# Two attention blocks on one core: block 2's keys and values as three float32r products, scores laid out by batch, output product moved behind the next pair's scores

## Chip, cores and metric

One Trainium2 chip, one of its cores. The metric is the device time of the kernel in microseconds (us), median of three runs. Five engines work side by side, each through its own list of instructions in order, and they wait for one another by semaphores: PE (matmuls; PEld is its weight load), DVE, ACT, POOL, and SP, which here only issues DMAs.

## What is computed

32 sequences of 64 tokens, width 128. A transformer block with 16 heads of width 8 (causal self-attention, attention to a context, a feed-forward part, three layer norms) is followed by one attention block with 16 heads of width 64, a bias `f` on the scores that counts twice, an output product and a layer norm. Block 2, which the change is about, cut to what matters:

```python
x = block1(x, ctx)                                   # 3 layer norms, small heads
qh = (x @ wq + bq) / 8;  kh = ctx @ wk + bk;  vh = ctx @ wv + bv     # 16 heads x 64
scores = qh @ kh.T + f + f                           # per batch and head, 64 x 64
ctx2 = softmax(scores) @ vh
out = layernorm(ctx2 @ wo + bo + x)                  # width 128
```

All data is fp32 in memory. Wq, wk, wv of block 2 are 128 x 1024.

## The kernel before

Two sequences make a pair (128 tokens, one per partition), so there are 16 pairs. Every pair goes through three chains of steps: A (self-attention and its layer norm), B (attention to the context, its layer norm, the feed-forward part and its layer norm) and C (block 2). A of one pair, B of an earlier one and C of a still earlier one run at the same time; A is five pairs ahead of C, B two to three.

**Order.** Each engine's list is written by one function, `run`, which goes through `PLAN`: the steps of all chains and pairs, sorted by pair number plus a place from the table `TURN` (`C.e=-1.106` and so on). An engine takes from it the steps that are its own. So the table alone sets the order on every engine, and once 11 or so pairs are in flight the same rows repeat for each pair. Between engines only semaphores (`s_...`) order the work.

**Banks.** A and B have three PSUM banks each (J, E, X). Chain C has two, `C.E[0]` and `C.E[1]`, each 128 x 512 fp32, and every product of C goes through them in turn: keys (`C.k_0`, `C.k_1`), values (`C.v_0`, `C.v_1`), the transposed input (`C.x3t`), queries (`C.q_0/1`), scores (`C.e`), transposed probabilities (`C.pt_0/1`), probabilities times values (`C.zt`) and output product (`C.o_0/1`).

**Chain C, step by step** (line of the kernel in brackets):
- `C.k_g` (L455): keys. For four pairs at a time one product of a 128 x 128 slice of wk with 512 columns of the transposed context; two of them in each pair's turn, four pairs ahead of their use. `C.ks_g` (ACT, L614) adds the bias and copies into `kT`.
- `C.v_b` (L469): values of batch b, in two products with 64 rows of output each and 512 columns; `C.vs_b` (ACT, L624) copies.
- `C.x3t`, `C.q_g` (L480, L488): queries; `C.qs_g` (ACT, L646) adds bias and scales by 1/8.
- `C.e` (L503): 32 products 64 x 64 x 64. It waits for `L4.s_y`: the addition `C.y` of the pair before has read the output product out of bank 0.
- Softmax: `C.fadd_g` (DVE, L837) computes 2f + scores from PSUM, `C.max_g` (DVE, L846), `C.sub_g` (POOL, L929), `C.exp_g` (ACT, L654), `C.den_g` (DVE, L854, L856), `C.nrm_g` (POOL, L938).
- `C.pt_g` (L514), which also waits for the queries of the next pair to be out of the banks, `C.pts_g` (ACT, L663), `C.zt` (L528), `C.zts_r` (ACT, L633), `C.o_r` (L537): eight products 128 x 128 x 128 that add up in 128 columns of bank 0.
- `C.y` (DVE, L865) adds x; then the layer norm of C: `C.st` (DVE), `C.rstd` (POOL), `C.xh` (DVE), `C.gb` (POOL), `store` (SP).

The same four names with A, B and B.3 before them are the other three layer norms (L795 and L799, L896 and L898, L808, L907 and L912). `A.kblk` and `B.kblk` (POOL, L888) spread the keys of block 1 over eight heads (128 x 1024); `A.e` and `B.e` (L365) wait for them and for `xh` of the pair before in the same chain. `B.f1`, `B.f2`, `B.f3` are the feed-forward part on PE.

SP issues all loads of weights and inputs first, then in turn `load_f` (512 KB of bias for a pair, two buffers) and the 64 KB store.

## Time and profile before

| | |
|---|---|
| median of the runs (3) | 397.06 us (396.39 to 400.57) |
| the profiled execution's own time | 397.58 us |
| its span in the profile | 395.4 us |
| around the span | 2.2 us |
| PE busy | 345.0 us (87%), 5296 matmul records |
| DVE, ACT, POOL busy | 293.4 (74%), 232.7 (59%), 235.7 (60%) us |
| HBM read / written | 15.99 / 1.05 MB |

The time is that of a whole execution, the span is from its first to its last recorded instruction. An fp32 matmul shows as two records in the trace, so a count is twice that of the program's. PE's ends are modelled and overlap: what a matmul costs in a full stream is read from the start of one group to the start of the next, not from its duration. The span has three parts: filling (until the first `C.e`, 77 us), a repeating middle, and emptying (no more A, then no more B) from about 299 us.

### The profile page before, as it was taken

The numbers are of one execution on the slowest core, as the hardware profiler recorded it, in microseconds if no ns is written. First come the engines' busy times: TensorE is split into PE (matmuls) and PEld (weight loads), VectorE is DVE, ScalarE is ACT, GpSimd is POOL, SyncE is SP. The second block draws the span as 40 slices with busy tenths as digits, with TensorE's granted clock in tenths as the row PEclk, the third lists the DMA queues.
The fourth block names the chain that finished last, engine by engine and source line by source line (L and its number), as shares of the span: only waits on it lengthen the run. The fifth ranks groups of instructions, "written<-read, shape, count | busy, mean of one in ns | idle before, by whom it ended". The sixth has DMA issues, their size and how long they took to land.

```text
span 395.4 us, 13051 instructions
## 1 busy us (share of the span) xinstructions
PE 345.0 (87%) x5296; PEld 240.2 (61%) x5296; DVE 293.4 (74%) x833; ACT 232.7 (59%) x561; POOL 235.7 (60%) x372
## 2 busy tenths in 40 slices
...
PEclk9968889999999999999999999999999999999955
...
GB/s 163 325 342 48 0 2 2 2 55 3 2 2 61 5 61 3 61 2 61 5 61 4 61 2 61 5 61 2 61 5 61 2 61 2 61 2 61 8 8 7
DMA packets 13178, 17.86 MB, mean 45 GB/s; under 512 B 1600, under 2 KB 10176, under 8 KB 13120
## 3 DMA queue, kind: packets, MB, share of 16 engines
...
q8 instruction: 42, 0.69, 0.7%
...
HBM read 15.99 MB, written 1.05 MB: 43 GB/s over the span
## 4 chain that ended last, share of the span: by engine, by line
PE 73%; POOL 8%; DVE 7%; ACT 6%; issue 4%; DMA 1%; SPq 1%; POOLq 0%; ACTq 0%; DVEq 0%
PE C_E L455 8%; PE C_E L537 7%; PE C_E L488 6%; PE C_E L469 6%; PE C_E L514 4%; PE C_E L528 4%; PE A_E L365 4%; PE C_E L503 3%; PE B_E L365 3%; PE A_E L398 2%; PE B_E L398 2%; PE B_E L384 2%; POOL B_kblk L888 2%; PE B_X L384 2%; PE A_X L384 2%
## 5 line engine op out<-in xcount | busy, mean ns | idle before, releaser
L568 ACT ACTIVATE A_S<-A_S 128x512 f32<-128x512 f32 x32 | 20.2, 631 | 65.8 <-DVE A_S L766 65.8
L888 POOL TENSOR_TENSOR A_kblk<-A_qk,cst 128x1024 f32<-128x1024 f32 x16 | 30.4, 1898 | 41.1 <-DVE A_qk L734 39.8
L896 POOL TENSOR_TENSOR L_ve<-L_mv,cst 128x1 f32<-128x1 f32 x64 | 12.3, 192 | 61.4 <-DVE L_mv L799 61.3
L929 POOL TENSOR_TENSOR Sc<-Sc,mxc 128x512 f32<-128x512 f32 x32 | 33.4, 1044 | 22.2 <-DVE mxc L846 22.2
L907 POOL TENSOR_TENSOR L_xg<-L_xh,vec_sb 128x128 f32<-128x128 f32 x64 | 29.4, 459 | 17.9 <-DVE L_xh L808 17.9
L898 POOL TENSOR_TENSOR L_rstd<-L_ve,cst 128x1 f32<-128x1 f32 x64 | 35.2, 551 | 5.0
L537 PEld LDWEIGHTS C_E<-wo_sb,C_zT 128*128 128x128 f32 x256 | 31.4, 200 | 11.1 <-ACT C_zT L633 11.1
L537 PE MATMUL C_E<-wo_sb,C_zT 128*128 128x128 f32 x256 | 34.6, 291 | 3.5 <-ACT C_zT L633 3.5
L455 PE MATMUL C_E<-cTs,wk_sb 128*128 128x512 f32 x64 | 36.0, 645 | 0.3 <-DVE Sc L837 0.3
L938 POOL TENSOR_TENSOR Pc<-Pc,rdc 128x512 f32<-128x512 f32 x32 | 33.0, 1045 | 4.8 <-DVE rdc L856 4.8
L646 ACT ACTIVATE qT<-C_E,bq 128x128 f32<-128x128 f32 x128 | 34.8, 384 | 0.7 <-PE C_E L488 0.7
L488 PE MATMUL C_E<-x3T,wq_sb 128*128 128x128 f32 x256 | 31.7, 277 | 0.4 <-ACT x3T L638 0.4
L469 PE MATMUL C_E<-wv_sb,cTs 128*64 128x512 f32 x128 | 31.2, 606 | 0.1
L488 PEld LDWEIGHTS C_E<-x3T,wq_sb 128*128 128x128 f32 x256 | 29.8, 191 | 1.0 <-ACT x3T L638 0.9
L888 POOL TENSOR_TENSOR B_kblk<-B_qk,cst 128x1024 f32<-128x1024 f32 x16 | 30.4, 1897 | 0.0
L633 ACT COPY C_zT<-C_E 128x512 f32<-128x512 f32 x32 | 17.2, 589 | 22.1 <-PE C_E L528 22.1
L854 DVE TENSOR_REDUCE denc<-Pc 128x8 f32<-128x512 f32 x32 | 21.8, 681 | 5.6 <-ACT Pc L654 5.5
L365 PE MATMUL A_E<-A_kblk,A_qk 64*64 64x512 f32 x64 | 19.4, 684 | 6.8 <-DVE L_xh L808 4.0
L514 PE MATMUL C_E<-cst,Pc 128*128 128x128 f32 x128 | 18.2, 286 | 8.1 <-POOL Pc L938 5.6
L654 ACT ACTIVATE Pc<-Sc 128x512 f32<-128x512 f32 x32 | 20.5, 640 | 8.0 <-POOL Sc L929 8.0
L837 DVE SCALAR_TENSOR_TENSOR Sc<-f,C_E 128x512 f32<-128x512 f32 x32 | 21.7, 679 | 4.1 <-PE C_E L503 4.1
L614 ACT ACTIVATE kT<-C_E,bk_sb 128x512 f32<-128x512 f32 x32 | 21.9, 685 | 2.0 <-PE C_E L455 2.0
...
## 6 DMA issues: line engine op xcount, KB each, us to landing
...
```

Of the source, the lines that this page charges most:

```text
L365: last = mm(bank[S * b:S * b + S, :], a.qk[r, 0, S * b:S * b + S], a.kblk[r, :, S * b:S * b + S], start=True, stop=not causal, skip_group_ ...
L455: mm(C.E[g][:, :], wk_sb[:, j * P:(j + 1) * P], cTs[:, group * FIRST * P:(group + 1) * FIRST * P], start=True, stop=True).then_inc(C.s_k, 1)
L469: last = mm(C.E[b][S * r:S * r + S, :], cTs[:, n * P + S * b:n * P + S * b + S], wv_sb[:, r], start=True, stop=True)
L488: last = mm(C.E[g][:, j * P:(j + 1) * P], wq_sb[:, c:c + P], x3T[:], start=True, stop=True)
L514: last = tr(C.E[g][:, j * P:(j + 1) * P], Pc[:, c:c + P], ident)
L537: last = mm(C.E[0][:, 0:D], zT[:, r, jj], wo_sb[:, 2 * jj + r], start=(r == jj == 0), stop=(r == 1 and jj == J // 2 - 1))
L646: last = act.activation(qT[:, 4 * g + j], C.E[g][:, j * P:(j + 1) * P], ACT.Identity, bias=bq8[:, 4 * g + j:4 * g + j + 1], scale=float(DK ...
L888: tt(a.kblk[:], a.qk[:, 1].unsqueeze(1).to_broadcast([P, 8, P]), at["rmask"].unsqueeze(2).to_broadcast([P, 8, P]), ALU.mult).then_inc(a.s_ ...
L898: tt(l.rstd[:], l.ve[:], at["power"], ALU.pow).then_inc(l.s_rstd, 1)
L907: tt(l.xg[:], l.xh[:], l.g, ALU.mult).then_inc(l.s_xg, 1)
L929: tt(v, v, mxc[:, 8 * g:8 * g + 8].unsqueeze(2).to_broadcast([P, 8, S]), ALU.subtract).then_inc(C.s_sub, 1)
L938: tt(pr, pr, rdc[:, 8 * g:8 * g + 8].unsqueeze(2).to_broadcast([P, 8, S]), ALU.mult).then_inc(C.s_nrm, 1)
```

## The change

It does five things.

1. `C.k_g` and `C.v_m`: weights and context are split into a high part (a copy to type float32r) and a low part (the difference, again float32r), and each product is made of three: high x high, low x high, high x low, accumulated in PSUM. The values are now computed for both batches at once, 128 output rows by 512 columns, in two halves of the heads. So per pair 12 matmuls of 128 x 128 by 512 columns in float32r stand in place of 2 of 128 x 128 and 4 of 128 x 64, all by 512 columns, in fp32.
2. The splits are new steps: once, `C.whi` and `C.wvhi` on ACT (128 x 1024 each), `C.wlo` and `C.wvlo` on DVE (128 x 1024 each); every four pairs, `C.chi` on ACT and `C.clo` on POOL (128 x 512 each).
3. Scores go to bank b for batch b (before: by head parity), probabilities and f are laid out to match (`by_half` on the host), and `C.zt`, `C.zts` and `C.o` follow. The numbers of matmuls stay. The doubling of f moves into the scale of the exponential, so `C.fadd` is a plain addition of the same size.
4. `C.e` of a pair no longer waits for `C.y` of the pair before, only for `C.zts`. `C.o` (one step now) waits for `C.fadd_1` of the next pair, which has read the banks; `C.k` and `C.v` wait for `C.y`.
5. All numbers of `TURN` are new.

```diff
-                        pe.wait_ge(C.s_s, 2 * (n - FIRST) + 1 + g)
-                    mm(C.E[g][:, :], wk_sb[:, j * P:(j + 1) * P], cTs[:, group * FIRST * P:(group + 1) * FIRST * P],
-                       start=True, stop=True).then_inc(C.s_k, 1)
+                        pe.wait_ge(C.s_s, 2 * (n - FIRST) + 2)
+                        if g == 0 and n > FIRST:
+                            pe.wait_ge(L4.s_y, n - FIRST)
+                    hi, lo = (w[:, j * P:(j + 1) * P] for w in (wk_hi, wk_lo))
+                    chi, clo = cT_hi[group % 2], cT_lo[group % 2]
+                    mm(C.E[g][:, :], hi, chi[:], start=True, stop=False)
+                    mm(C.E[g][:, :], lo, chi[:], start=False, stop=False)
+                    mm(C.E[g][:, :], hi, clo[:], start=False, stop=True).then_inc(C.s_k, 1)
...
-                    for r in range(2):
-                        last = mm(C.E[b][S * r:S * r + S, :], cTs[:, n * P + S * b:n * P + S * b + S], wv_sb[:, r],
-                                  start=True, stop=True)
-                    last.then_inc(C.s_v, 1)
+                    mm(C.E[m][:, :], chi, hi, start=True, stop=False)
+                    mm(C.E[m][:, :], chi, lo, start=False, stop=False)
+                    mm(C.E[m][:, :], clo, hi, start=False, stop=True).then_inc(C.s_v, 1)
...
                 pe.wait_ge(C.s_qs, 2 * n + 2)
                 if n:
-                    pe.wait_ge(L4.s_y, n)
+                    pe.wait_ge(C.s_zts, 2 * n)
...
-                            last = mm(C.E[hl][S * b:S * b + S, j * S:(j + 1) * S], qT[r, j, S * b:S * b + S],
+                            last = mm(C.E[b][S * (hl ^ b):S * (hl ^ b) + S, j * S:(j + 1) * S], qT[r, j, S * b:S * b + S],
...
+            def c_o(n):
+
+                pe.wait_ge(C.s_zts, 2 * n + 2)
+                if n + 1 < PAIRS:
+                    pe.wait_ge(C.s_s, 2 * n + 4)
+                for j in range(J):
+                    last = mm(C.E[0][:, 0:D], zT[:, j].rearrange("p b c -> p (b c)"), wo_sb[:, j], start=(j == 0), stop=(j == J - 1))
+                last.then_inc(C.s_o, 1)
...
+                act.wait_ge(w_keys, 16 * 3)
+                act.copy(wk_hi[:], wk_sb[:]).then_inc(C.s_whi, 1)
...
+                act.copy(cT_hi[n // FIRST % 2][:], cTs[:, n * P:(n + FIRST) * P]).then_inc(C.s_chi, 1)
...
+                dve.wait_ge(C.s_whi, 1)
+                tt(wk_lo[:], wk_sb[:], wk_hi[:], ALU.subtract).then_inc(C.s_wlo, 1)
...
-                    dve.scalar_tensor_tensor(sc, f[n % 2][:, g * HALF:(g + 1) * HALF], 2.0,
-                                             C.E[g][:, :], ALU.mult, ALU.add).then_inc(C.s_s, 1)
+                    e = C.EE[:].rearrange("p (b j t) -> p j b t", b=2, t=S)[:, 4 * g:4 * g + 4]
+                    tt(sc.rearrange("p (j b t) -> p j b t", b=2, t=S),
+                       f[n % 2][:, g * HALF:(g + 1) * HALF].rearrange("p (j b t) -> p j b t", b=2, t=S), e, ALU.add
+                       ).then_inc(C.s_s, 1)
...
-                dve.wait_ge(C.s_o, 2 * n + 2)
+                dve.wait_ge(C.s_o, n + 1)
...
-C.zts_1=-0.1903111 C.o_0=-0.1675396 C.o_1=-0.1404375 C.st=0.1958135 C.xh=0.2584186 C.rstd=0.3205016
+C.zt=-0.1529242 C.o=0.1188686 C.st=0.2670199 C.rstd=0.3155987 C.gb=0.4200828 C.xh=0.5391835
```

The order on PE in the repeating middle, from `C.zt` (L528) of one pair past `C.e` (L503) of the next, before:

```order
L528 MATMUL C_E<-PTc,C_V 64x64 x32
L365 MATMUL A_E<-A_kblk,A_qk 64x512 x2
L365 MATMUL A_X<-A_kblk,A_qk 64x512 x2
L372 MATMUL A_E<-later,eye 64x512 x2
L372 MATMUL A_X<-later,eye 64x512 x2
L537 MATMUL C_E<-wo_sb,C_zT 128x128 x8
L324 MATMUL A_J<-xTs,Wq_sb 128x128
L325 MATMUL A_J<-xTs,Wk_sb 128x128
L329 MATMUL A_J<-Wv_sb,xTs 64x64 x4
L503 MATMUL C_E<-kT,qT 64x64 x32
L365 MATMUL B_E<-B_kblk,B_qk 64x512 x2
L365 MATMUL B_X<-B_kblk,B_qk 64x512 x2
```

The same stretch of the change (`C.zt` is L542, `B.e` L374, `B.f1` L438, `C.e` L520, `C.o` L552):

```order
L542 MATMUL C_E<-PTc,C_V 64x64 x32
L374 MATMUL B_E<-B_kblk,B_qk 64x512 x2
L374 MATMUL B_X<-B_kblk,B_qk 64x512 x2
L438 MATMUL B_J<-cst,x 128x128
L520 MATMUL C_E<-kT,qT 64x64 x32
L348 MATMUL A_J<-A_q,A_qk 64x16 x2
L445 MATMUL B_J<-x2T,fc1T_sb 128x128
L393 MATMUL A_E<-cst,A_S 128x128 x4
L393 MATMUL A_X<-cst,A_S 128x128 x4
L450 MATMUL B_J<-fc2T_sb,hT 128x128
L552 MATMUL C_E<-wo_sb,C_zT 128x128 x8
L407 MATMUL A_E<-A_PT,A_V 32x64 x16
```

The output product has moved from ahead of the next pair's scores to behind them, with five short steps of A and B between; `B.e` and `B.f1` have moved ahead of the scores, `A.e` ahead of `C.pt`.

DVE at the very start of the program (`A_mx` is the maximum of pair 0's scores in chain A, `A_S` the subtraction of it), before:

```order
L758 TENSOR_REDUCE A_mx<-A_E 128x8
L758 TENSOR_REDUCE A_mx<-A_X 128x8
L766 TENSOR_TENSOR A_S<-A_E,A_mx 128x512
L766 TENSOR_TENSOR A_S<-A_X,A_mx 128x512
L713 TENSOR_TENSOR A_q<-cst,A_J 128x32
```

and in the change:

```order
L805 TENSOR_REDUCE A_mx<-A_E 128x8
L805 TENSOR_REDUCE A_mx<-A_X 128x8
L728 TENSOR_TENSOR wk_lo<-wk_sb,wk_hi 128x1024
L813 TENSOR_TENSOR A_S<-A_E,A_mx 128x512
L813 TENSOR_TENSOR A_S<-A_X,A_mx 128x512
```

`wk_lo`, which needs wk from HBM and its high part from ACT, stands between the maximum and the subtraction of the first pair.

POOL in the repeating middle (`Pc<-Pc,rdc` is `C.nrm`, a pair of `L_ve`, `L_rstd` one `rstd`, `L_xg` with the row after it one `gb`), before:

```order
L888 TENSOR_TENSOR A_kblk<-A_qk,cst 128x1024
L938 TENSOR_TENSOR Pc<-Pc,rdc 128x512 x2
L896 TENSOR_TENSOR L_ve<-L_mv,cst 128x1
L898 TENSOR_TENSOR L_rstd<-L_ve,cst 128x1
L896 TENSOR_TENSOR L_ve<-L_mv,cst 128x1
L898 TENSOR_TENSOR L_rstd<-L_ve,cst 128x1
L922 TENSOR_TENSOR x3r<-h_3,obias 128x128
L907 TENSOR_TENSOR L_xg<-L_xh,vec_sb 128x128
L912 TENSOR_TENSOR x_1<-L_xg,vec_sb 128x128
```

and in the change:

```order
L994 TENSOR_TENSOR Pc<-Pc,rdc 128x512
L945 TENSOR_TENSOR L_ve<-L_mv,cst 128x1
L947 TENSOR_TENSOR L_rstd<-L_ve,cst 128x1
L937 TENSOR_TENSOR A_kblk<-A_qk,cst 128x1024
L956 TENSOR_TENSOR L_xg<-L_xh,vec_sb 128x128
L961 TENSOR_TENSOR x_1<-L_xg,vec_sb 128x128
L994 TENSOR_TENSOR Pc<-Pc,rdc 128x512
L937 TENSOR_TENSOR B_kblk<-B_qk,cst 128x1024
L945 TENSOR_TENSOR L_ve<-L_mv,cst 128x1
L947 TENSOR_TENSOR L_rstd<-L_ve,cst 128x1
L945 TENSOR_TENSOR L_ve<-L_mv,cst 128x1
L947 TENSOR_TENSOR L_rstd<-L_ve,cst 128x1
```

The two `C.nrm` are apart, `A.rstd` stands ahead of `A.kblk`, and `B.kblk` ahead of `B.rstd` and `C.rstd`.

## Rows read from the trace of the kernel before

**Rows 1.** The page: TensorE clock in 40 slices; engines' shares of the chain.

```profile
PEclk9968889999999999999999999999999999999955
...
PE 73%; POOL 8%; DVE 7%; ACT 6%; issue 4%; DMA 1%; SPq 1%; POOLq 0%; ACTq 0%; DVEq 0%
```

**Rows 2.** Busy time by stretch, 160 to 180 us.

```profile
core 0: us, PE busy (x) PEld busy (x) DVE busy (x) ACT busy (x) POOL busy (x), PEclk, DMA share, GB/s
...
160.00:180.00 20.00, 19.96 (x338) 14.26 (x331) 17.58 (x52) 14.26 (x36) 14.61 (x24) 1.00 0.11 32
```

**Rows 3.** Timeline of PE: start, us, engine, line, op, tiles; parts of five stretches.

```profile
76.90 1.16 PE L503 MATMUL C_E<-kT,qT 64*64 64x64 f32 x64
...
98.74 1.16 PE L503 MATMUL C_E<-kT,qT 64*64 64x64 f32 x64
...
161.03 1.02 PE L455 MATMUL C_E<-cTs,wk_sb 128*128 128x512 f32 x2
161.90 0.38 PE L436 MATMUL B_J<-x2T,fc1T_sb 128*128 128x128 f32 x2
...
163.53 1.12 PE L455 MATMUL C_E<-cTs,wk_sb 128*128 128x512 f32 x2
164.59 1.94 PE L469 MATMUL C_E<-wv_sb,cTs 128*64 128x512 f32 x8
166.46 0.69 PE L398 MATMUL A_E<-A_PT,A_V 128*32 128x64 f32 x32
...
176.12 2.05 PE L537 MATMUL C_E<-wo_sb,C_zT 128*128 128x128 f32 x16
178.00 0.39 PE L324 MATMUL A_J<-xTs,Wq_sb 128*128 128x128 f32 x2
...
178.93 1.16 PE L503 MATMUL C_E<-kT,qT 64*64 64x64 f32 x64
...
299.00 1.16 PE L503 MATMUL C_E<-kT,qT 64*64 64x64 f32 x64 [0.43 <-issue]
...
371.59 2.05 PE L537 MATMUL C_E<-wo_sb,C_zT 128*128 128x128 f32 x16 [0.71 <-ACT C_zT L633]
374.07 1.16 PE L503 MATMUL C_E<-kT,qT 64*64 64x64 f32 x64 [0.43 <-issue]
```

**Rows 4.** Groups of PE by form: mean ns of one (bf16 ones from 100:280).

```profile
L372 PE MATMUL A_E<-later,eye 64*64 64x512 bf16 x18 | 3.5, 376 | 0.0
...
L353 PE MATMUL A_J<-ofb,A_nz 128*128 128x2 bf16 x9 | 1.5, 168 | 0.0
...
L537 PEld LDWEIGHTS C_E<-wo_sb,C_zT 128*128 128x128 f32 x256 | 31.4, 200 | 11.1 <-ACT C_zT L633 11.1
```

**Rows 5.** Timeline of DVE, 160 to 181 us: the rows with idle time before them.

```profile
168.88 0.26 DVE L776 RECIPROCAL A_rd<-A_X 128x16 f32<-128x16 f32 x1 [0.41 <-PE A_X L409]
...
172.25 0.19 DVE L713 TENSOR_TENSOR B_q<-cst,B_J 128x32 f32<-128x32 f32 x1 [0.66 <-ACT B_qk L561]
...
173.43 0.29 DVE L721 TENSOR_SCALAR B_nz<-B_J 128x128 bf16<-128x128 f32 x1 [0.42 <-PE B_J L339]
```

**Rows 6.** Groups of POOL by form: busy us, mean ns of one.

```profile
L898 POOL TENSOR_TENSOR L_rstd<-L_ve,cst 128x1 f32<-128x1 f32 x64 | 35.2, 551 | 5.0
...
L888 POOL TENSOR_TENSOR A_kblk<-A_qk,cst 128x1024 f32<-128x1024 f32 x16 | 30.4, 1898 | 41.1 <-DVE A_qk L734 39.8
```

**Rows 7.** The start: SP's issue of bq, its time to landing, DVE's first subtraction.

```profile
10.90 0.43 SPq L273 DMA_DIRECT2D bq_sb<-in_bq  x1
...
bq_sb<-in_bq SPq DMA_DIRECT2D x1, 4.0 KB, 4.8
...
15.32 0.68 DVE L766 TENSOR_TENSOR A_S<-A_E,A_mx 128x512 f32<-128x512 f32 x1
```

**Rows 8.** Timeline of PE after the last scores.

```profile
380.62 1.12 PE L514 MATMUL C_E<-cst,Pc 128*128 128x128 f32 x4 [5.39 <-POOL Pc L938]
...
386.42 3.79 PE L537 MATMUL C_E<-wo_sb,C_zT 128*128 128x128 f32 x16 [0.70 <-ACT C_zT L633]
```

More of the change, by code:

```diff
@@ L50 @@
 HALF = H * S // 2
+QSCALE = 0.5 * float(DK1) ** -0.5
 EPS0, EPS1 = 1e-5, 1e-6
@@ L57, with by_half @@
 CONST = dict(ident=P, hmask=H, rmask=H // 2, bsel=2, trow=1, own=2, power=1, eps0=1, eps1=1)
-LATE = np.array([2 * j + hl for hl in range(2) for j in range(J)])
+def by_half(fs):
+    f = fs.reshape(PAIRS, 2, J, 2, S, S)
+    halves = [np.stack([f[:, b, :, c ^ b] for b in range(2)], axis=2) for c in range(2)]
+    return np.stack(halves, axis=1).transpose(0, 1, 4, 2, 3, 5).reshape(B * S, H * S)
 def constants():
@@ L202, in bass_two_blocks @@
         C.s_k = sem("C_k")
+        C.s_chi, C.s_clo, C.s_whi, C.s_wlo = (sem("C_" + n) for n in ("chi", "clo", "whi", "wlo"))
         C.s_ks = sem("C_ks")
@@ L664, in c_pts @@
                 return step
-            steps = {"B.cm": b_cm, "B.xts": xts, "B.f1s": f1s, "B.f2s": f2s, "C.x3ts": x3ts}
+            steps = {"B.cm": b_cm, "B.xts": xts, "B.f1s": f1s, "B.f2s": f2s, "C.x3ts": x3ts, "C.whi": whi, "C.wvhi": wvhi,
+                     "C.chi": chi}
             for nm, a in (("A", A), ("B", Bc)):
@@ L940, in nrm @@
                 return step
-            steps = {"C.x3c": x3c, "C.sub_0": c_sub(0), "C.sub_1": c_sub(1), "C.nrm_0": nrm(0), "C.nrm_1": nrm(1),
+            steps = {"C.x3c": x3c, "C.clo": clo, "C.sub_0": c_sub(0), "C.sub_1": c_sub(1), "C.nrm_0": nrm(0), "C.nrm_1": nrm(1),
                      "A.kblk": kblk(A), "B.kblk": kblk(Bc),
@@ L956 @@
 TURN = """
-C.loadf=-6.3703055 A.q0=-6.3054844 A.nz=-6.1218368 A.qkv=-6.1094448 A.kblk=-6.0420715 A.qk=-6.0184605
-A.cut=-5.8655348 A.e0=-5.8129968 A.m0=-5.7641686 A.v=-5.7500991 C.store=-5.6244090 A.cnt=-5.5866611
-A.max_0=-5.5821687 A.max_1=-5.5178588 A.sub_0=-5.5031429 A.sub_1=-5.3952696 A.e=-5.2258359 A.exp_0=-5.1750322
-C.k_0=-5.0297461 A.exp_1=-4.9916915 A.pt_0=-4.8885878 A.pt_1=-4.8746226 C.ks_0=-4.8690466 A.zn=-4.8606247
-A.y=-4.8313232 A.st=-4.8098507 C.k_1=-4.8078464 A.pts_0=-4.8067054 A.rstd=-4.7877968 A.pts_1=-4.7811586
@@ L977 @@
-C.gb=0.7617832
+C.loadf=-13.6882109 C.store=-12.6575872 A.m0=-6.8598273 A.q0=-6.4320183 A.qk=-6.2393158 A.qkv=-6.1876511
+A.nz=-6.1197152 A.kblk=-6.0915634 A.e0=-6.0767926 A.cut=-6.0114914 A.v=-5.9787105 C.whi=-5.9401554
+A.cnt=-5.7244213 A.max_0=-5.6253244 C.clo=-5.5908806 A.max_1=-5.5582182 C.wlo=-5.5064165 A.sub_0=-5.4982827
+A.sub_1=-5.4755154 A.e=-5.2973272 C.chi=-5.2111519 A.exp_0=-5.1535699 A.zn=-5.1030891 A.rstd=-5.0985058
+A.y=-5.0913649 A.exp_1=-5.0900544 A.st=-5.0504854 A.pts_0=-5.0305842 A.pts_1=-5.0305806 A.pt_0=-5.0119762
```

144 lines of the change are left out of this document (85 added, 59 removed).

## The prediction

> **What bounds the kernel now.** I began with the chain that ended last and the clock by slices: 73% of the chain lies on PE, and from the seventh slice to the 38th the granted clock is 9 tenths or more, so the middle runs at the upper of PE's two levels (2.4 GHz), and the last two slices, at 5, at the lower (1.2 GHz) [rows 1]. Then the busy time of one stretch of the middle: PE is busy 19.96 of 20 us, DVE 17.58, POOL 14.61, ACT 14.26 [rows 2]. PE there waits for nobody. The timeline gives the period: the scores of C start at 98.74 and 178.93 us, four pairs apart, so a pair costs 80.19 / 4 = 20.05 us; from 98.74 to 299.00 ten pairs pass, 20.03 each [rows 3]. The span falls into filling (76.9 us to the first scores), a first interval of 98.74 - 76.90 = 21.84, ten intervals of 20.03, emptying of 374.07 - 299.00 = 75.07 for four pairs, and an end of 395.4 - 374.07 = 21.3 [rows 3].
>
> DVE is the second to look at. Its 17.58 leaves out the small gaps between instructions. In a period it sits idle, waiting for another engine, 0.41 + 0.66 + 0.42 = 1.49 us [rows 5]; so it needs 20.05 - 1.49 = 18.56 us a pair. A faster PE can save 1.5 us a pair at most before DVE is the bound.
>
> **PE: keys and values.** Keys of a pair cost 161.90 - 161.03 = 0.87 and 164.59 - 163.53 = 1.06, values 166.46 - 164.59 = 1.87: 3.80 us [rows 3]. In their place come 12 float32r products of 512 columns. No row shows float32r. An fp32 product of 512 columns takes 0.87, the dearer end. For one pass through the array I take the bf16 records: 512 columns last 376 ns, 2 columns 168 ns [rows 4], so 510 columns stream in 0.21 us; four such make 0.84, close to the 0.87 of fp32, which therefore is four passes. float32r at one pass is 0.21, at two 0.42, at four 0.87. I take one pass plus a little for the issue, 0.22, because three products in place of one would otherwise be dearer than what they replace; that is a choice and not a reading, so 0.21 and 0.87 both stay ends of the range. 12 x 0.22 = 2.64, so PE saves 3.80 - 2.64 = 1.16 us a pair and needs 18.9.
>
> The Trainium skill's page FP8 and Floating Point Precision, section TensorE Precision Notes, has it that true fp32 takes four passes, and that its "FP32 reduced precision" reads the four bytes and truncates; it gives no pass count for the latter, so only the first half is borne out here (0.87 against 0.84).
>
> The weights: a load of 128 x 128 fp32 takes 200 ns [rows 4], yet the output product's 16 records, each with its own load, pass in 178.00 - 176.12 = 1.88 us, 0.12 a record [rows 3]. Loads hide behind running products, and I cost the 12 new ones at nothing; uncovered they would add 12 x 0.20 = 2.4 us a pair. The Trainium skill, TensorE: Matmul & The Clock Gate, in Part 3 under what overlaps, says that a weight load overlaps running matmuls only when its row group differs. All 12 new products use all rows, so by that rule the 2.4 would be paid. The output product uses all rows too, and the trace disagrees. The rule's result is part of rival three.
>
> **Other edits in the middle.** `C.fadd` stays one DVE pass over 512 elements from PSUM (a two-operand pass of that size from PSUM, L766, takes 0.68 us [rows 7]), though it now reads two banks in pieces of 64: zero, with +-0.05 a pass. Scores, `C.zt` and `C.o` keep their counts: zero. `chi` and `clo` are one 128 x 512 copy and one subtraction every four pairs, on engines at 14.3 and 14.6 of 20 [rows 2]: zero while these have room. SP's order puts each f load ahead of a store it stood behind: SP moves 512 KB in a tenth of its time [rows 2], zero; if that cover failed, `C.fadd` would wait.
>
> **The order in the middle.** Moving `C.o` behind the next scores takes `C.y` out of the loop scores - softmax - `zt` - scores. PE was full, so this buys nothing by itself; it lets PE keep its 18.9 instead of waiting. I laid the new rows of all engines along durations of the trace for one period, zero at `C.e`. `fadd_1` ends at 2.5, `C.o` runs 2.6 to 4.5, `C.y` comes after `max_1` at 5.4, `k_0` at 5.7: fits. `C.x3t` at 9.9 needs the layer norm of B.3, ready at 9.2: fits. `A.xh` waits on DVE 0.25 for `A.rstd`, which stands behind a `nrm` on POOL. `B.nz` waits 0.35 for `B.e0`. Last, POOL does `B.kblk` (1.90), then `B.rstd` and `C.rstd` (0.55 each with its 0.2 ahead), then `B.gb` [rows 6]; `B.kblk` cannot start before 14.9, because `nrm_1` and `A.gb` are ahead. So `B.xh` waits 0.25 on DVE, and behind it stand the subtractions of A, the maxima of B and then the next `fadd`; and `B.gb` ends at 19.3, which frees `B.f1` and behind it on PE `C.e`, at 19.4. The three DVE waits make 18.56 + 0.85 = 19.4 as well. DVE and POOL together now set the period, not PE. I take 19.4, bounds 18.9 (PE alone) and 20.0 (no gain). Ten intervals: 10 x (20.03 - 19.4) = -6.3. The first interval, 21.84, I put at 20.4, one more than the others: -1.4.
>
> **Filling.** ACT's `whi` waits until bq has landed, 10.90 + 4.8 = 15.7 us [rows 7], and copies 1024 columns; I put 1.2 for it and 1.2 for DVE's `wk_lo`, estimates from two passes of 512 at a little under L766's 0.68. `wk_lo` ends at 18.1. DVE's first subtraction, now behind it, started at 15.32 [rows 7]: +2.8 us for chain A's first pair, and everything of A queues behind it. The next three turns of A carry `k` between `A.pv` and `A.z`, and `A.rstd` ahead of `A.kblk`; each puts up to 1 us on the loop of A. Against it, PE's keys and values, at the lower clock in part, are cheaper by a quarter, about 2 us over the filling. Sum +3, bounds 0 and +5.
>
> **Emptying.** There PE has gaps, and the chain of C itself sets the pace: in the last interval `C.o` at 371.59 stands between `zts` and `C.e` at 374.07, 2.48 us [rows 3]. These go from each of four intervals. In return `x3t` of the next pair comes later: `B.f3`'s result is taken up by DVE only after `max_1` and `C.y`. I count 1.4 net, 4 x 1.4 = -5.6.
>
> **End.** After the last scores PE was idle 5.39 us before `C.pt`, and the granted clock fell to its lower level: eight products of `C.o` took 3.79 us against 1.88 [rows 8, 3]. In the change `C.o` of pair 14 fills the start of this gap and leaves some 2.4. If the clock holds, `C.pt`, `C.zt` and `C.o` take about 3 us less; if not, nothing. I take the middle, -1.5.
>
> **Sum.** -6.3 - 1.4 + 3 - 5.6 - 1.5 = -11.8 on the profiled execution's 397.58: 385.8. That execution lies 0.5 above the median of 397.06, so on the median's footing 385.3.
>
> **Rivals.**
> 1. *PE stays the bound.* DVE's waits vanish in its idle time. For: PE was full and every other engine has room on the average [rows 2]. Against: DVE needs 18.56 with no wait at all. Period 18.9: -11.3, first interval -1.9, filling +1, emptying -6.5, end -2: -20.7, time 376.4.
> 2. *The order gives back what the products save.* The waits of DVE for POOL feed on one another, period 20.0. For: DVE leaves only 1.49 us of play and POOL's rows stand later. Against: the walk finds three short waits. Filling +3, emptying -5, end -1, first interval -1: -4.3, time 392.8. This is within what the change would do if it saved PE time to no end.
> 3. *float32r is dearer than one pass.* Two passes at 0.42, or one with its weight load uncovered, 0.21 + 0.20 = 0.41. Then 12 x 0.42 = 5.04 against 3.80, PE at 21.3 a pair: +12.5 over ten intervals, +1 in the first, filling +4, emptying -4, end -1.5: +12, time 409. It ends slower than before, and decides from a product cost of about 0.35 us (3.80 / 12 = 0.32 breaks even on PE alone; the emptying pays for the rest). Against: 0.12 a record in the output product, loads included. For: no row shows the type. Four passes (the split buys nothing) would be 12 x 0.87 = 10.4, +6.6 a pair, time near 480; I give it 1 in 100.
>
> **Chances.** Forecast 0.50, rival one 0.20, rival two 0.15, rival three 0.12, the rest 0.03. The likeliest alone has 380 to 391. The range, 375 to 395, takes in rivals one and two and leaves three out. A measurement of this kernel tells about 1% from no change, 4 us. Faster by over 1% (below 393.1) is forecast, rival one and some of two: 0.78. Within 1%: the rest of two and a little: 0.10. Slower by over 1%: 0.12.
>
> **What would show it.** In the trace after: starts of `C.e` 19.4 apart; float32r records stepping by 0.22; PE busy near 19 of 19.4 with short waits before `C.e` or `B.f1` for POOL's x; DVE's idle down to under 1 us a period; first `C.e` near 80 us; `C.e` 14 to 15 about 16 apart; an idle gap of about 2.4 before the last `C.pt`. The prediction is wrong if a float32r product steps by over 0.3, if the period falls below 19.0 or stays at 20, or if the first scores come later than 82.

## The result and the profile after

| | before | changed |
|---|---|---|
| median of the runs, us | 397.19 (396.39 to 400.57, 4 runs) | 405.87 (404.80 to 406.24, 4 runs) |
| ratio, 95% interval | | 1.020 (1.014 to 1.026) |
| span of the profiled execution, us | 395.4 | 403.8 |
| granted clock, mean | 0.956 | 0.929 |

The change makes the kernel 2% slower; 385.3 us was forecast, with a range up to 395. Ratios here and below leave out runs more than 1.5% above the fastest of the same kernel. The clock by slices and the chain that ended last, from the page of the changed kernel:

```profile
PEclk9975997989999999999999999999999999968665
PE 63%; POOL 15%; DVE 9%; issue 5%; ACT 5%; DMA 1%; SPq 1%; POOLq 0%; ACTq 0%; DVEq 0%
```

Against [rows 1] the clock is lower in the fourth slice (5 in place of 8), the seventh and ninth (7 and 8 in place of 9) and the 36th to 38th (6, 8, 6 in place of 9 each); the third, fifth, sixth and 39th are a step higher. PE's share of the chain has gone from 73% to 63%, POOL's from 8% to 15%. Busy time in one stretch of the middle and in one of the emptying:

```profile
core 0: us, PE busy (x) PEld busy (x) DVE busy (x) ACT busy (x) POOL busy (x), PEclk, DMA share, GB/s
160.00:180.00 20.00, 19.80 (x338) 15.70 (x334) 17.93 (x54) 15.83 (x39) 16.31 (x25) 1.00 0.11 32
356.00:368.00 12.00, 9.95 (x153) 8.77 (x154) 3.63 (x8) 2.48 (x6) 3.37 (x6) 0.57 0.03 7
```

The middle is as full as in [rows 2]. From 356 to 368 us PE runs at little over half its clock; behind that it changes between the two levels. The starts of the scores (`C.e`, L520) show where the time went, against [rows 3]:

| stretch | before | after | difference | forecast |
|---|---|---|---|---|
| filling, to the first `C.e` | 76.90 | 86.53 | +9.6 | +3 |
| first interval | 21.84 | 20.03 | -1.8 | -1.4 |
| ten intervals | 200.26 | 195.72 | -4.5 | -6.3 |
| emptying, four intervals | 75.07 | 77.38 | +2.3 | -5.6 |
| end, behind the last `C.e` | 21.3 | 24.1 | +2.8 | -1.5 |

The differences sum to +8.4, as the spans do. The middle did about what was said. The loss is in the first 87 and in the last 100 us. The middle first, in the timeline of PE:

```profile
start us, us, engine line op out<-in xcount [idle before <-releaser]
170.94 0.47 PE L468 MATMUL C_E<-cT_hi,wk_hi 128*128 128x512 f32 x1
171.25 0.39 PE L469 MATMUL C_E<-cT_hi,wk_lo 128*128 128x512 f32 x1
171.48 0.39 PE L470 MATMUL C_E<-cT_lo,wk_hi 128*128 128x512 f32 x1
171.71 0.38 PE L418 MATMUL A_X<-cst,A_zT 128*128 128x128 f32 x2
```

The starts, not the durations of the overlapping records, give the price: 171.25 - 170.94 = 0.31 for the first product of a set, then 0.23 and 0.23. A set of three is 0.77, the four sets of a pair 3.08 us in place of 3.80 [rows 3]. The filling, on DVE:

```profile
9.46 0.69 DVE L751 TENSOR_REDUCE am<-xs 128x4 f32<-128x512 f32 x1 [2.25 <-DMA xs<-in_x]
...
10.26 0.18 DVE L760 TENSOR_TENSOR A_q<-cst,A_J 128x32 f32<-128x32 f32 x1
...
17.95 1.22 DVE L728 TENSOR_TENSOR wk_lo<-wk_sb,wk_hi 128x1024 fp32r<-128x1024 f32 x1
19.08 0.68 DVE L813 TENSOR_TENSOR A_S<-A_E,A_mx 128x512 f32<-128x512 f32 x1
...
57.38 1.50 DVE L734 TENSOR_TENSOR wv_lo<-wv_sb,wv_hi 128x1024 fp32r<-128x1024 f32 x1
58.80 0.67 DVE L751 TENSOR_REDUCE am<-xs 128x4 f32<-128x512 f32 x1
...
59.67 0.28 DVE L768 TENSOR_SCALAR B_nz<-B_J 128x128 bf16<-128x128 f32 x1
```

Three things stand in DVE's list ahead of work that chain A or B waits for: the maximum over |xs| (`A.m0`), which waits for its load; the split of the key weights; the split of the value weights with the next maximum, for which PE waits 2.19 us before L360 at 60.00. And the emptying, on PE:

```profile
359.36 1.99 PE L520 MATMUL C_E<-kT,qT 64*64 64x64 f32 x64 [0.82 <-issue]
...
363.12 3.62 PE L552 MATMUL C_E<-wo_sb,C_zT 128*128 128x128 f32 x16
...
383.13 3.75 PE L552 MATMUL C_E<-wo_sb,C_zT 128*128 128x128 f32 x16 [1.49 <-DVE Sc L885]
...
394.83 3.78 PE L552 MATMUL C_E<-wo_sb,C_zT 128*128 128x128 f32 x16 [1.19 <-ACT C_zT L667]
```

Before, PE was at its upper clock until 376 us; here the output product, whose record lasted 2.05 us [rows 3], takes 3.62 us already at 363.

### The profile page after: what moved, and what is told of

The parts are those of the page before. It is cut to its first block, busy times and chain, and to the rows that moved or that the text cites. A ratio compares the mean times of both kernels' runs of the same rounds, so it can differ in the third digit from the quotient of the medians.

```text
span 403.8 us, 13090 instructions
## 1 busy us (share of the span) xinstructions
PE 343.6 (85%) x5296; PEld 268.1 (66%) x5296; DVE 291.9 (72%) x835; ACT 244.9 (61%) x567; POOL 241.9 (60%) x376
## 3 DMA queue, kind: packets, MB, share of 16 engines
HBM read 15.99 MB, written 1.05 MB: 42 GB/s over the span
## 4 chain that ended last, share of the span: by engine, by line
PE 63%; POOL 15%; DVE 9%; issue 5%; ACT 5%; DMA 1%; SPq 1%; POOLq 0%; ACTq 0%; DVEq 0%
PE C_E L552 8%; PE C_E L505 7%; POOL B_kblk L937 6%; PE C_E L520 5%; POOL L_rstd L947 3%; PE A_E L407 2%; PE B_E L393 2%; PE B_E L407 2%; PE C_E L468 2%; PE A_E L393 2%; PE A_E L374 2%; PE C_E L470 2%; PE C_E L469 2%; PE C_E L486 2%; PE C_E L488 2%
## 5 line engine op out<-in xcount | busy, mean ns | idle before, releaser
L680 ACT ACTIVATE qT<-C_E,bq 128x128 f32<-128x128 f32 x128 | 36.4, 370 | 17.2 <-PE C_E L505 17.2
L937 POOL TENSOR_TENSOR A_kblk<-A_qk,cst 128x1024 f32<-128x1024 f32 x16 | 30.4, 1898 | 15.6 <-DVE A_qk L781 15.6
L552 PE MATMUL C_E<-wo_sb,C_zT 128*128 128x128 f32 x256 | 36.7, 304 | 2.9 <-DVE Sc L885 1.5
L552 PEld LDWEIGHTS C_E<-wo_sb,C_zT 128*128 128x128 f32 x256 | 34.8, 218 | 3.8 <-issue 2.2
L956 POOL TENSOR_TENSOR L_xg<-L_xh,vec_sb 128x128 f32<-128x128 f32 x64 | 30.3, 473 | 11.4 <-DVE L_xh L855 11.4
L505 PE MATMUL C_E<-x3T,wq_sb 128*128 128x128 f32 x256 | 35.1, 281 | 0.6 <-ACT x3T L672 0.6
L885 DVE TENSOR_TENSOR Sc<-f,C_E 128x512 f32<-128x512 f32 x32 | 20.5, 684 | 16.1 <-PE C_E L520 15.2
L505 PEld LDWEIGHTS C_E<-x3T,wq_sb 128*128 128x128 f32 x256 | 30.9, 191 | 1.4 <-ACT x3T L672 1.0
L697 ACT COPY PTc<-C_E 128x512 f32<-128x512 f32 x32 | 17.3, 588 | 16.2 <-PE C_E L531 16.2
L374 PE MATMUL A_E<-A_kblk,A_qk 64*64 64x512 f32 x64 | 19.9, 702 | 6.3 <-POOL A_kblk L937 6.3
L531 PEld LDWEIGHTS C_E<-cst,Pc 128*128 128x128 f32 x128 | 13.7, 141 | 16.7 <-POOL Pc L994 10.8
L542 PE MATMUL C_E<-PTc,C_V 64*64 64x64 f32 x1024 | 20.7, 236 | 4.3 <-ACT PTc L697 4.3
```

Of the source, the lines that this page charges most:

```text
L374: last = mm(bank[S * b:S * b + S, :], a.qk[r, 0, S * b:S * b + S], a.kblk[r, :, S * b:S * b + S], start=True, stop=not causal, skip_group_ ...
L505: last = mm(C.E[g][:, j * P:(j + 1) * P], wq_sb[:, c:c + P], x3T[:], start=True, stop=True)
L531: last = tr(C.E[g][:, j * P:(j + 1) * P], Pc[:, c:c + P], ident)
L552: last = mm(C.E[0][:, 0:D], zT[:, j].rearrange("p b c -> p (b c)"), wo_sb[:, j], start=(j == 0), stop=(j == J - 1))
L680: last = act.activation(qT[:, 4 * g + j], C.E[g][:, j * P:(j + 1) * P], ACT.Identity, bias=bq8[:, 4 * g + j:4 * g + j + 1], scale=QSCALE)
L937: tt(a.kblk[:], a.qk[:, 1].unsqueeze(1).to_broadcast([P, 8, P]), at["rmask"].unsqueeze(2).to_broadcast([P, 8, P]), ALU.mult).then_inc(a.s_ ...
```

## The experiments

Most are the changed kernel with some rows of its order moved ("`A.m0(0)` -6.86 to -5.97": the step stands at the place of that number). The kernel before itself spread from 392.98 to 402.87 us in the runs made beside these experiments (medians 398.6 to 401.9). So where there is one run only, the intervals of its trace are read, and its total with 5 us of doubt either way. The changed kernel was not measured again beside them: what is "under the changed kernel" compares with the four runs above.

**1. The new arithmetic in the old order.**

```
TURN: that of before; C.o whole, C.k and C.v at their old places
+ C.chi -5.18, C.clo -5.195, C.whi -4.78, C.wlo -4.744, C.wvhi -2.27, C.wvlo -2.1508
+ k_0(0) -4.1, k_1(0) and ks_0(0) -4.09, ks_1(0) -4.085
C.e(n) waits for C.y(n - 1); C.o does not wait for C.fadd
```

> The change's arithmetic (float32r products, splits, scores by batch, one C.o) in the order and with the waits of the kernel before: C.o ahead of the next C.e, C.e waits for C.y; the splits of the weights stand where their engines were idle, keys of pair 0 one turn of A later. Theory order: the change loses in its new order at the start and at the end, the products themselves save 0.7 us a pair. Then first C.e within 2 us of 76.9, period 19.3 to 19.5, last interval as before, total 386 to 391 us. Rival clock: float32r products themselves let TensorE's clock fall in filling and emptying. Then first C.e later than 80 us, emptying over 76 us with stretches of clock 0.5 before 374 us, total 396 or more.

Measured: 433.5 us (431.74 to 434.26), ratio 1.094 (1.084 to 1.104). Period, last interval and total missed; the start did not: the first `C.e` comes at 74.94 us, where 76.9 was expected and the change has 86.53. So the new products and the splits, put where their engines wait, cost nothing in the filling; what is lost there comes with the order. But `C.e` comes every 21.76 us, and every fourth interval takes about 25. PE's waits:

```profile
148.69 0.50 PE L468 MATMUL C_E<-cT_hi,wk_hi 128*128 128x512 f32 x1 [1.62 <-DVE Sc L883]
...
171.60 0.80 PE L468 MATMUL C_E<-cT_hi,wk_hi 128*128 128x512 f32 x1 [2.78 <-POOL cT_lo L976]
```

The second is my own placing of `clo` (a POOL pass of 1.27 us behind a softmax pass). The first is in the change: with the scores by batch, keys half 0 waits until DVE has read both banks of scores; before it waited for one. So the new order isn't a free choice beside the arithmetic.

**2. That wait alone, in the kernel before.**

```
-                        pe.wait_ge(C.s_s, 2 * (n - FIRST) + 1 + g)
+                        pe.wait_ge(C.s_s, 2 * (n - FIRST) + 2)
```

> The kernel before with one wait made later: keys half 0 (C.k_0) waits for both halves of the scores of four pairs earlier to be read by VectorE (it waited for the first), as scores by batch makes it wait. Theory, from the run with the old order: this in-order wait of 1.6 us per pair, with f1 and A.pt queued behind it on TensorE, is what the change's new order was needed for; C.e comes every 21.7 us instead of 20.06, and the whole takes 417. Rival: VectorE's second read of the scores lies so close that the wait costs less than 0.5 us per pair, and the old order failed for another reason: under 405.

Measured: 420.8 us, one run; from 97.75 to 294.84 nine intervals of 21.90 against 20.03, and

```profile
167.34 1.12 PE L455 MATMUL C_E<-cTs,wk_sb 128*128 128x512 f32 x2 [1.57 <-DVE Sc L837]
```

The theory holds: 1.57 us of wait, 1.87 us of period. In the changed kernel the same wait shows no idle time in the middle, since `k_0` stands later: there the new order does its work.

**3. One fp32 product in place of three float32r**, in the changed kernel.

```
-                    mm(C.E[g][:, :], hi, chi[:], start=True, stop=False)
-                    mm(C.E[g][:, :], lo, chi[:], start=False, stop=False)
-                    mm(C.E[g][:, :], hi, clo[:], start=False, stop=True).then_inc(C.s_k, 1)
+                    mm(C.E[g][:, :], wk_sb[:, j * P:(j + 1) * P], cTs[...], start=True, stop=True).then_inc(C.s_k, 1)
```

and the values likewise; the splits are still made, and not used.

> The change with its three float32r products in one fp32 product each (128 x 128 by 512, from the unsplit operands); splits still run, their results unused; same order, same waits. It prices float32r: a product of fp32 steps by 0.87, three float32r ones by 0.77, so the period goes from 19.57 to about 20.0, PE full again. Theory order: first C.e as late as in the change (86 to 88), emptying as slow (76 to 78), low clock there too; total 408 to 411. Rival clock: with fp32 products the clock holds in the emptying, C.e 12 to 15 come 18 apart or less, and total falls to 402 or less in spite of the longer period.

Measured: 416.4 us, one run; of the expectation the start holds (first `C.e` at 87.49); period, emptying (79.6 us) and total are above it. The intervals are 20.23 (189.25 to 290.39, five) against 19.57. From `C.e` to L360, the first row behind the four products, PE takes 199.30 - 189.25 = 10.05 us, and 174.68 - 165.28 = 9.40 in the change. The products are 0.65 us a pair dearer on PE, and the period is 0.66 longer. PE is as busy as in the change:

```profile
160.00:180.00 20.00, 19.80 (x326) 14.66 (x326) 17.29 (x51) 15.19 (x36) 15.77 (x24) 1.00 0.10 32
```

So PE still sets the period, and not DVE with POOL. And 20.23 is 0.17 above the 20.06 of the same stretch before: what the middle gains, it gains by the products; the new order by itself gains nothing there.

**4. The start moved.**

```
A.m0(0) -6.86 to -5.97    whi -5.94 to -5.03    wlo -5.51 to -4.969
k_0(0) -4.82 to -4.29     k_1(0) -4.78 to -4.285     ks_0(0), ks_1(0) to -4.16, -4.155
```

> The change with five steps of the first pair moved: A.m0 behind A.cut on DVE, whi behind A.pts_1 on ACT, wk_lo behind A.xh on DVE, k_0 and k_1 of pair 0 behind the second A.e on PE. Nothing else moves. Theory order: A.m0 (waits for xs) cost 2.6 us, wk_lo 1.2 and k ahead of A.z 1 to 2 of the filling: first C.e at 80 to 82.5 us in place of 86.5, total 400 to 402. Rival clock: the start is late because PE is at the lower level; first C.e stays at 85 or later.

Measured: 396.9 us, one run, first `C.e` at 82.08. Then its parts apart: `A.m0(0)` alone, the split with the keys of pair 0, and these keys alone (the split can't move without them, since it would wait for what waits for it).

> The changed kernel with one row moved: A.m0 of the first pairs (VectorE's maximum over |xs|, which waits for the load of xs until 9.46 us) behind A.v(0) instead of ahead of A.q0(0). With all start rows moved the kernel took 396.9 us against 405.9. Theory of added delays: the first A.e starts at 11.7 instead of 14.29 and every later step of the filling comes 2.6 us earlier, the first C.e at 84 and the whole at 403. Rival, the clock: the gain of the moved start comes mostly from the granted clock in the filling and in the last 50 us, which depends on how the stalls fall; then the interval starts of the emptying change too (17.6 and 18.1 us as with all rows moved, or 18.3 and 20.3 as in the changed kernel), and the time is 399 or 406.

> The changed kernel with the split of the key weights (ACT's wk_hi, VectorE's wk_lo) behind the first pair's softmax, and keys of pair 0 (k_0, k_1 and their copies to SBUF) behind A.e of pair 1; A.m0 stays where the change has it. Theory of added delays: the first A.e stays at 14.3, the second comes at 28.0 instead of 29.7 (wk_lo's 1.2 us out of A's chain), the first C.e at 84.5, the whole at 403.5, and with the run of A.m0 alone the two gains add up to the 9 us of all rows together only if the emptying runs at the full clock in each. Rival, the clock decides: the last three intervals sum to 56 us (granted clock near 1.0 until 360 us) and the time is under 401.

> The changed kernel with only keys of pair 0 moved behind A.e of pair 1; wk_hi and wk_lo stay ahead of A's softmax on ACT and VectorE. Theory: k_0(0) between A.pv and A.z of pair 0 runs at half clock and waits for the kT copies behind it, about 1.5 us; the first C.e comes at 85 and the whole takes 404.3. Rival: the keys of pair 0 lie beside the wait for kblk and cost nothing: 405.9, first C.e at 86.5.

Measured, one run each: 405.0, 398.1 and 407.8 us. Starts of `A.e` of the first three pairs, and of the first `C.e`:

| kernel | A.e | A.e | A.e | C.e |
|---|---|---|---|---|
| before | 11.66 | 24.25 | 37.12 | 76.90 |
| changed | 14.29 | 29.71 | 44.33 | 86.53 |
| `A.m0(0)` moved | 11.35 | 29.42 | 44.13 | 86.38 |
| split and keys moved | 14.75 | 28.05 | 43.44 | 84.75 |
| keys moved | 14.56 | 30.12 | 45.51 | 87.80 |
| all moved | 11.38 | 25.28 | 40.76 | 82.08 |

Delays don't simply add. `A.m0` alone brings the first energies 2.9 us earlier and the second 0.3; its trace says why, first ACT, then DVE:

```profile
15.64 1.04 ACT L624 CAST wk_hi<-wk_sb 128x1024 fp32r<-128x1024 f32 x1 [8.61 <-DMA bq_sb<-in_bq]
```

```profile
16.71 1.23 DVE L728 TENSOR_TENSOR wk_lo<-wk_sb,wk_hi 128x1024 fp32r<-128x1024 f32 x1 [1.62 <-ACT wk_hi L624]
17.86 0.68 DVE L813 TENSOR_TENSOR A_S<-A_E,A_mx 128x512 f32<-128x512 f32 x1
```

The split waits for a load at 15.6, and chain A behind it. While it is there, what is gained ahead of it is lost again; all rows together give 4.4 us at the first `C.e`.

The last column tells less than it seems to, because the filling is not the same from one execution to the next. Four traces have the changed kernel's order up to there (its own and those of experiments 6, 8 and 9): 86.53, 87.31, 86.77 and 87.65. Two have "split and keys moved" (this one and experiment 9's second kernel): 84.75 and 88.06. The kernel before has 76.90, 76.95 in experiment 6 and 72.42 in experiment 2, whose edit acts only behind the first `C.e`. In the two "split and keys" traces PE has the same rows up to there, but not at the same clock; so the transposition of A's first pair, in this one and in experiment 9's:

```profile
20.08 0.66 PE L393 MATMUL A_E<-cst,A_S 128*128 128x128 f32 x4
```

```profile
20.29 1.11 PE L393 MATMUL A_E<-cst,A_S 128*128 128x128 f32 x4 [0.22 <-ACT A_S L581]
```

From there the second `A.e` comes at 28.05 or 29.30, the third at 43.44 or 46.02. So these single traces don't tell what the split and the keys cost apart from each other; 87.8 with the keys alone moved is within what the changed kernel shows itself. With all rows moved the first `C.e` is earlier than in any trace of the changed kernel's order.

**5. The value split and the second maximum moved too.**

```
experiment 4, and: wvhi(0) -3.01 to -3.24   wvlo(0) -2.89 to -3.1045   A.m0(4) -2.86 to -2.047
```

> All start rows moved as in the run that took 396.9, and also the split of the value weights (VectorE's wv_lo, 1.50 us) into VectorE's wait before the reciprocal of A's third pair and the |xs| maximum of pairs 4 to 7 (0.9 us) behind B's first layer norm. Theory: B.nz of pair 1 comes 2.2 us earlier (54.2 instead of 56.4) and so the fifth A.e and the first C.e: 80 instead of 82.1, the whole 394.8. Rival: the turn that this shortens is bound elsewhere (PE A.z to A.kblk), the first C.e stays at 82 and the time at 397.

Measured: 399.4 us (397.94 to 401.34, 10 runs), ratio to before 1.009 (1.004 to 1.014); 6.5 us under the changed kernel. `B.nz`, at 56.09 with the start alone, starts at 53.54, and the first `C.e` at 80.31, so the filling does what the theory says: 3.4 us above before, where the change has 9.6. In the two other traces with these rows (experiments 7 and 9) it comes at 83.21 and 80.17. The total missed its 394.8. The clock took some back: the first interval is 20.27 (19.45 in experiment 4) with a granted clock of 0.83 from 80 to 90 us where that had 1.00, and pair 12 to 13 takes 20.61 (19.23).

**6. TensorE kept busy at the end.** The kernel before with 20 idle matmuls behind its last scores; the changed one with 34 in six waits of its last two pairs.

```
+                if n == PAIRS - 1:
+                    pe.wait_ge(L1.s_xh, PAIRS)
+                    for _ in range(20):
+                        mm(A.X[:, :], A.nz[:], later[:].unsqueeze(1).to_broadcast([P, 8, S]), start=True, stop=True)
```

> The kernel before with 20 matmuls added that compute nothing that is used (bf16, 128x512, into a bank that nothing reads any more), on TensorE behind the scores of the last pair, where it waits 5.4 us for the softmax. Theory: the low clock of the last 20 us is a price of TensorE's waits, and with the gap filled the transposes, the PV product and the output product of the last pair run at 1.00: the last L537 group takes 2.0 us instead of 3.8, PV 1.2 instead of 2.0, so the whole is 3.3 us shorter, 394 against 397. Rival: the clock is low there whatever the engine does, or the added matmuls end after Pc is ready and stand in the way: 397 or more.

> The changed kernel with 34 added matmuls whose result nothing uses, in TensorE's waits of pairs 14 and 15 (5 behind each C.q_1, 7 behind C.v_1, 5 behind C.e, 8 behind C.o of pair 14, 4 behind the last PV product). Theory: part of the loss is the granted clock of the last 50 us: from C.e of pair 14 (359.36) to the end the changed kernel takes 44.4 us, at clocks from 0.50 to 1.00, and the run with the split and the keys moved took 39.8 us with the same instructions; with the waits filled the last output product takes 2.0 us instead of 3.8 and the stretch comes to 38 to 39 us, the whole to 400. Rival: the clock falls ahead of the first added matmul (0.56 at 356 us) and the added ones, at half speed, stand in the way of the real ones: 405 or more.

Measured: before with them 394.6 us (391.56 to 398.34, 4 runs), ratio 0.989 (0.976 to 1.002), unclear as a total; in its trace the end is 18.3 us against 21.3, and the last output product takes 2.05 us where [rows 8] has 3.79:

```profile
385.14 2.05 PE L541 MATMUL C_E<-wo_sb,C_zT 128*128 128x128 f32 x16 [0.70 <-ACT C_zT L637]
```

Changed with them: 398.9 (396.11 to 400.69, 10 runs), 7.0 under the changed kernel. From `C.e` of pair 14 to the end it takes 37.1 us (360.95 to 398.1) against 44.4. The mean granted clock of its ten runs is 0.961 to 0.973, that of the changed kernel's four 0.928 to 0.949. Two stretches and two products of it:

```profile
356.00:368.00 12.00, 8.85 (x167) 6.79 (x166) 5.47 (x13) 4.76 (x12) 6.21 (x12) 1.00 0.02 7
368.00:380.00 12.00, 8.81 (x168) 6.14 (x167) 2.77 (x8) 5.47 (x15) 4.95 (x10) 1.00 0.03 7
```

```profile
363.60 2.02 PE L568 MATMUL C_E<-wo_sb,C_zT 128*128 128x128 f32 x16
...
380.77 2.02 PE L568 MATMUL C_E<-wo_sb,C_zT 128*128 128x128 f32 x16 [0.30 <-DVE Sc L905]
```

The granted clock is 1.00 where the changed kernel had 0.57, and the output product 2.02 us in place of 3.62 and 3.75. In the first stretch that is only in part the added matmuls' doing: without any, it had 0.86 and 0.92 in experiment 4 (all moved; split and keys moved). The products behind the last scores are the plain case: in every trace without added matmuls the last output product lasts 3.4 to 3.8 us, in the four with them 1.99 to 2.19. Work that computes nothing makes the kernel faster: there the low clock came from PE's waits.

**7. Both.** Experiment 5 with the matmuls of experiment 6.

> Both: the start rows moved, wv_lo and the maximum of pairs 4 to 7 too, and the 34 filling matmuls of pairs 14 and 15. Theory: the two gains add, since one is in the first 80 us and the other in the last 45: first C.e at 80, 299.5 us of steady and emptying stretch, end about 38 us behind C.e of pair 14; 389 to 391, under the kernel before (397) by 2%. Rival: the clock in the emptying was already 1.00 until 360 us with the start moved, so that the filling matmuls give only the last product's 1.8 us and the PV product's 0.8: 392 to 394.

Measured: 392.0 us (389.24 to 393.64, 6 runs), ratio to before 0.988 (0.981 to 0.995). The gains add: 405.9 less 6.5 less 7.0 is 392.4. Among experiments 5 to 7 alone, which were measured together, the matmuls are worth 399.4 - 392.0 = 7.4 us and the start rows 398.9 - 392.0 = 6.9. Its emptying is at 1.00 throughout and takes 372.78 - 299.19 = 73.59 us, its end 18.9.

**8. The output product of the late pairs at its old place**, from pair 11 on, ahead of the next scores, with `C.y` and `C.x3c` moved along.

> The change, but from pair 11 on C.o stands ahead of the next C.e again (on PE, with C.y ahead of the next fadd on DVE, C.e waiting for C.y), as in the kernel before. Theory: in the emptying, C.y waits for C.o in DVE's list ahead of the denominators and of the layer norm of B.3, so moving C.o behind the scores lengthens the softmax by what it takes out ahead of them; put back, C.e 12 to 15 come no later and the end after the last C.e falls from 24.1 to 21 to 22 us: total 402 to 404. Rival: C.o ahead costs its 2.4 us a pair, emptying 4 to 8 us longer, total 410 or more.

Measured: 418.4 us, one run. The rival's total came, but not by its price of 2.4 us a pair: the intervals from pair 11 on are 21.95, 24.40, 22.12 and 23.52 us, longer than the change's by 2.4, 5.2, 3.8 and 3.2, with the clock down to 0.63 in the last. Like experiment 1 it says that one piece of the order can't be put back alone. It doesn't say what the output product's place is worth.

**9. `C.y` of pairs 11 to 13 behind B's statistics** on DVE: on the changed kernel, on that with split and keys moved, and on experiment 7 (with 2 matmuls instead of 7 behind `C.v_1`).

```
C.y(11), C.y(12), C.y(13): n - 0.157 to n - 0.135
```

> The changed kernel with one row of VectorE moved in three pairs: L_y (C.y of pairs 11, 12 and 13, which waits for the output product) behind B.y3 and the statistics of B's third layer norm (of pairs 13, 14, 15) instead of ahead of them. Theory: in the emptying the output product, now inside the next pair's softmax, holds up B.y3 through VectorE's list, and with it h, the queries and the next scores, by 2.0 to 2.5 us in each of the last two intervals at full clock; the last two intervals come to 33.5 us against 38.6 here (17.6 and 18.1 at full clock), and the time to 401. Rival: the chain from B.f3 to the queries is as long without it, since TensorE's values of pair 15 and the output product come first anyway: the last intervals stay within 0.5 us and the time at 405.

> The same move of L_y on top of the kernel with the key split and the first keys moved (398.07 us; its last four intervals 19.56, 19.24, 17.63, 18.27, nearly all at full clock). Theory: 17.63 becomes 15.6 and 18.27 becomes 16.2, from C.e of pair 13 (338.7) to C.e of pair 15 in 31.9 us instead of 35.9, the time 394. Rival: within 0.5 us of the same intervals, 398.

> All start rows moved, the filling matmuls (2 instead of 7 behind C.v_1, since the wait there should shrink), and the move of L_y: the version meant to be fastest. Theory: 392.0 less 4 us of the two last intervals, 388. Rival: 392, if the L_y row costs nothing, or 396 and more, if the clock falls ahead of pair 14.

Measured: 403.6 and 404.7 us, one run each, and 392.8 (390.52 to 394.29, 6 runs), ratio 0.990 (0.983 to 0.997). DVE behind the scores of pair 14, first in the changed kernel (`C.e` at 359.36), then in the last (at 353.69):

```profile
366.77 0.29 DVE L914 TENSOR_TENSOR L_y<-C_E,x3r 128x128 f32<-128x128 f32 x1 [2.90 <-PE C_E L552]
366.98 0.29 DVE L870 TENSOR_TENSOR B_J<-B_J,vec_sb 128x128 f32<-128x128 f32 x1
```

```profile
357.30 0.29 DVE L890 TENSOR_TENSOR B_J<-B_J,vec_sb 128x128 f32<-128x128 f32 x1
357.62 0.36 DVE L892 SCALAR_TENSOR_TENSOR B_J<-B_J,m0s,x 128x128 f32<-128x128 f32 x1
358.01 0.30 DVE L862 BATCH_NORM_STATS2 L_st<-B_J 128x6 f32<-128x128 f32 x1
...
358.45 0.29 DVE L934 TENSOR_TENSOR L_y<-C_E,x3r 128x128 f32<-128x128 f32 x1
```

B's row (L870, then L890) comes 7.62 us behind the scores there and 3.61 here. At full clock the change's order of rows has it at 361.27 - 356.35 = 4.9 (experiment 4, split and keys moved), so part of the 7.62 is the clock. The last interval, at 1.00 in both, is 16.11 against 17.16 in experiment 7: the row is worth 1.05 us, not 2.0 to 2.5. The five matmuls fewer behind `C.v_1` have no part in it, since in both traces PE waits 0.32 us behind them for POOL's `h`. Pair 13 to 14 stays at 17.63. In the total nothing can be told: the clock fell to 0.57 at 332 us and again in the last `C.e`.

The second kernel here holds all the rows of the one that took 398.1, moves one more in three pairs, and took 404.7. Of these 6.7 us, 4.1 lie ahead of the second `C.e`, where the two have the same rows (experiment 4). The rest lies in the emptying and the end, with a clock of 0.57 from 356 to 368 where the other had 0.92:

```profile
356.00:368.00 12.00, 9.98 (x157) 8.95 (x157) 4.21 (x10) 3.31 (x7) 5.44 (x10) 0.57 0.03 7
```

So the single runs of experiments 4 and 9 don't rank kernels; the sets of 6 and 10 runs (experiments 5, 6, 7 and 9) do.

## Why the prediction was wrong, step by step

- **PE: keys and values.** Mis-sized. A float32r product steps by 0.23, and 0.31 at the head of a set, not 0.22: 3.08 us in place of 2.64, a saving of 0.72 and not 1.16. One pass a product was the right choice, and no weight load showed: 12 uncovered ones would have made 2.4 us a pair more. By the rule of the Trainium skill, TensorE: Matmul & The Clock Gate, Part 3, they would have been paid; the measurement decides against it here.
- **The order in the middle.** The size was nearly right, 19.57 against 19.4, the reason was not. PE sets the period (experiment 3), as rival one had it; my chain of DVE and POOL waits was not the limit. I had PE's need too low (18.9) and a limit that wasn't one (19.4), and the two errors met near the right number: that is luck. From 20.03 - 0.72 = 19.3 another 0.27 us is missing, and no run says where it lies. Ten intervals gave -4.5 of -6.3, the first -1.8 of -1.4.
- **Scores by batch: "zero".** In the changed order this holds. It failed as a cost by itself: in the order of before the wait for both banks costs 1.87 us a pair (experiment 2), more than the cheaper products save. I had costed the edit by its instructions and not by who waits for its end.
- **Filling: +3.** This step failed, by 6.6 us. I had `whi`'s wait for bq and `wk_lo` (15.7 and 18.1 against 15.37 and 19.08 measured), but not `A.m0` ahead of `A.q0` (its wait for xs to 9.46), nor `wv_lo` and the second maximum ahead of `B.nz` (2.2 us). The order is the cause (experiment 1: 74.94 with the same products and splits). The claim that cheaper products give 2 us back found nothing: with fp32 products the first `C.e` comes at 87.49, against 86.53 to 87.65 with float32r (experiments 3 and 4). With these rows moved the filling is 3.3 to 6.3 above the 76.9 of before (experiments 5, 7, 9). What is left shows first between the second and third `A.e` (15.4 to 17.0 us against 12.9). The candidates are the keys of pair 0, which now stand there for 2.2 us on PE ahead of the next products of A, the keys of pair 1 between `A.pv` and `A.z`, and `A.rstd` ahead of `A.kblk`; no run tells them apart. How much each moved row is worth by itself stays open too, since one filling differs from the next by up to 3.3 us with the same rows.
- **Emptying: -5.6.** This step failed, by 7.9 us. The 2.48 us of `C.o` did leave the loop, but at full clock (experiment 7) the four intervals took 73.6 against 75.1: -1.5. Pair 13 to 14 gained 1.3, the other three differ by 0.2 or less. The step took 1.1 of the 2.48 us as given back in each interval; in three of the four nearly all of it was. In the last one `C.o` holds up B's rows through `C.y` in DVE's list (1.05 us, experiment 9); what gives it back in the others was not tested. The other 3.8 us went with the granted clock, of which the step had no word: it was 0.57 from 356 to 368 us and is 1.00 there with the waits filled.
- **End: -1.5.** The wait before the last `C.pt` did shrink, to 2.33 us as forecast (2.4), and the clock did not hold: I took the middle between "holds" and "nothing", and had no side for a clock that falls earlier. It was +2.8; the size of 3 was also read too large, since the 1.88 beside 3.79 is a distance of starts and the record itself lasts 2.05. With the waits filled the end is 18.9 in the new order and 18.3 in the old.
- **Rivals.** One was right on the bound of the middle. Two had the order give back what the products save, but in the middle, where it did not; its filling (+3) and emptying (-5) missed as well. Three (dearer products) was wrong in its cause, and that its 409 lies near the measured time is luck. Of the prediction's own signs of being wrong the first scores behind 82 us came.
